# First weights from ScalarE's queue, products by quarter for two tiles, squares in column tiles, merged semaphores in the generator

## The reference, cut to what matters

```python
# layer 0
scale = cond @ norm_w.T + 1.0
h = x * (scale[:, None, :] * rsqrt(mean(x * x) + 1e-6))
val, gate = split(h @ up_w.T)            # 2 x 1024 columns
h = val * gelu(gate)
y = act_quant(h) @ weight_quant(down_w).T + x
# layer 1: gamma * rmsnorm(x) + beta goes into attention, and again into
# silu(x @ gate_w.T) * (x @ hidden_w.T) @ out_w.T + out_b
```

## Time and profile before

| | us |
|---|---|
| median of 3 runs | 745.24 (744.87 to 746.19) |
| the profiled execution | 745.31 |
| its span | 743.5 |
| TensorE busy, share of the span | 98% |
| VectorE, ScalarE, GpSimd busy | 69%, 49%, 55% |

### The profile page before, as it was taken

The page is one execution under the profiler, slowest core; times in us unless marked ns, Lnnn a source line. Parts: engine busy times, 40 slices in busy tenths (PEclk is TensorE's granted clock), DMA queues, the critical chain, the costliest instruction groups (busy, mean ns, idle before and its releaser), DMA issues.

```text
span 743.5 us, 18090 instructions
## 1 busy us (share of the span) xinstructions
PE 728.1 (98%) x6406; PEld 596.1 (80%) x6406; DVE 515.2 (69%) x806; ACT 361.3 (49%) x721; POOL 410.6 (55%) x408
## 2 busy tenths in 40 slices
PE   8999999999999899999999999999999999999996
PEld 7788888888888799999998777777777767778884
DVE  3987777777789889888985464646655567454467
ACT  3544443444447687888875333333333332322585
POOL 4646545555678888999987624224242423320344
PEclk9999999999999999999999999999999999999998
DMA  8954443454433010000004355577757777769953
GB/s 277 272 108 107 107 107 101 103 120 120 102 71 72 15 34 3 2 1 0 2 4 121 98 173 177 175 229 207 209 172 257 206 218 234 235 166 387 386 179 129
DMA packets 81002, 105.71 MB, mean 142 GB/s; under 512 B 39824, under 2 KB 53296, under 8 KB 80816
## 3 DMA queue, kind: packets, MB, share of 16 engines
q1 hardware_dynamic: 79792, 103.33, 47.2%
q10 hardware_dynamic: 1152, 1.59, 0.8%
HBM read 75.24 MB, written 21.26 MB: 130 GB/s over the span
## 4 chain that ended last, share of the span: by engine, by line
PE 89%; DVE 3%; POOL 3%; DMA 2%; issue 2%; ACT 1%; SPq 0%; DVEq 0%; POOLq 0%; ACTq 0%
PE banks L1283 22%; PE banks L440 22%; PE banks L1313 12%; PE banks L1129 5%; PE banks L1335 4%; PE banks L1206 4%; PE banks L521 4%; PE banks L1164 3%; PE banks L1247 3%; PE banks L1222 2%; PE banks L1944 2%; PE banks L1188 2%; PE banks L1914 2%; DMA qt<-q 1%; DMA early<-in_up_t 1%
## 5 line engine op out<-in xcount | busy, mean ns | idle before, releaser
L620 ACT ACTIVATE gelu<-banks,rstd 128x512 f32<-128x512 f32 x64 | 44.0, 688 | 116.5 <-PE banks L440 114.8
L1665 DVE TENSOR_TENSOR g<-banks,silu 128x512 f32<-128x512 f32 x64 | 44.1, 690 | 78.9 <-PE banks L1283 49.4
L1505 ACT ACTIVATE g_hi<-g 128x512 fp32r<-128x512 f32 x64 | 40.4, 631 | 96.9 <-DVE g L1665 95.9
L1669 DVE TENSOR_TENSOR g_lo<-g,g_hi 128x512 fp32r<-128x512 f32 x64 | 54.5, 852 | 47.5 <-ACT g_hi L1505 47.5
L1499 ACT ACTIVATE silu<-banks 128x512 f32<-128x512 f32 x64 | 38.2, 597 | 96.7 <-PE banks L1283 96.7
L440 PE MATMUL banks<-up_hi,xs_hi 128*128 128x512 f32 x256 | 81.9, 401 | 1.4 <-POOL xs_lo L370 0.8
L440 PE MATMUL banks<-up_lo,xs_hi 128*128 128x512 f32 x256 | 79.0, 391 | 0.4 <-DVE up_lo L774 0.4
L440 PE MATMUL banks<-up_hi,xs_lo 128*128 128x512 f32 x256 | 79.2, 391 | 0.0
L1283 PE MATMUL banks<-mlp_in_hi,w_hi 128*128 128x512 f32 x252 | 78.8, 393 | 0.0
L1283 PE MATMUL banks<-mlp_in_lo,w_hi 128*128 128x512 f32 x252 | 78.0, 391 | 0.0
L1283 PE MATMUL banks<-mlp_in_hi,w_lo 128*128 128x512 f32 x252 | 77.8, 390 | 0.0
(11 more groups left out here) (224 smaller groups left out, 1791.9 us busy)
## 6 DMA issues: line engine op xcount, KB each, us to landing
gen_hyper<-in_gen_t SPq DMA_DIRECT2D x32, 512.0 KB, 4.5
gen_made<-base_w SPq DMA_DIRECT2D x64, 256.0 KB, 4.6
adapter_w<-gen_made SPq DMA_DIRECT2D x64, 256.0 KB, 4.4
tokens<-in_x_tok SPq DMA_DIRECT2D x32, 128.0 KB, 2.3
w_stage<-in_w_t SPq DMA_DIRECT2D x32, 128.0 KB, 2.5
tokens_again<-in_x_tok SPq DMA_DIRECT2D x32, 128.0 KB, 2.3
weight_slot<-adapter_w SPq DMA_DIRECT2D x4, 1024.0 KB, 8.9
x_sb<-in_x_t SPq DMA_DIRECT2D x7, 512.0 KB, 7.0
```

The source lines that it names most:

```text
L620: nc.scalar.activation(gelu[:, j, :], up_bank(s, j, 1)[:, :], ACT.Gelu, scale=rstd0[:, bass.ds(s.at(0), 1)]).then_inc(Z["gelu_done"], 1)
L1505: nc.scalar.activation(gs[0][:, f % 2, :], g[:, f % 2, :], ACT.Copy).then_inc(S["g_hi_done"], 1)
L1665: nc.vector.tensor_tensor(g[:, f % 2, :], chunk_bank(s, f, 1)[:, :], silu[:, f % 2, :], ALU.mult).then_inc(S["g_done"], 1)
L1669: nc.vector.tensor_tensor(gs[1][:, f % 2, :], g[:, f % 2, :], gs[0][:, f % 2, :].bitcast(FP32), ALU.subtract).then_inc(S["g_ready"], 1)
```

## The change

The first up piece is loaded as two quarters by ScalarE's queue, together with the two small conditioning loads; SyncE begins with the tokens and the second piece. TensorE's first products go by these quarters, and the second tile's products move forward. The warm-up products are 7 and 9 instead of 14 and 7. ScalarE squares the first tokens behind the second piece, not the first.

```diff
-        sp.dma_start(cond_t[:], io["cond_t"]).then_inc(Z["loaded_norm"], 16)
-        sp.dma_start(cond_w[:, NORM * P:(NORM + 1) * P], ...).then_inc(Z["loaded_norm"], 16)
         load_x(0, 256, "loaded_x0")
-        load_up(0)
+        load_up(1)
         load_tokens(first[0])
-        load_up(1)
         load_up(2)
         load_up(3)
...
+    def load_first_up(act):
+        act.dma_start(cond_t[:], io["cond_t"]).then_inc(Z["loaded_norm"], 16)
+        act.dma_start(cond_w[:, NORM * P:(NORM + 1) * P], ...).then_inc(Z["loaded_norm"], 16)
+        for d, loaded in enumerate((Z["loaded_first"], loaded_up[0])):
+            act.dma_start(up_f[:, d, AT0:AT0 + 512], io["up_t"][:, d, AT0:AT0 + 512]).then_inc(loaded, 16)
...
+        pe.wait_ge(Z["xs_hi_done"], 1)
+        for d in range(DH):
+            pe.wait_ge(Z["up_hi_done"], d + 1)
+            nc.tensor.matmul(up_bank(first, J0, PART0)[:, :], xs_hi[:, 0, d, :], up[0][:, d, AT0:AT0 + 512], start=d == 0, stop=False)
         pe.wait_ge(Z["xs_ready"], 1)
-        pe.wait_ge(Z["up_hi_done"], 1)
-        with_high(first, 0)
+        up_product(first, 0, 1, 0, False, False)
...
         pe.wait_ge(Z["xs_ready"], 2)
         with_high(second, 0)
+        with_low(second, 0)
+        pe.wait_ge(Z["up_hi_done"], DONE0 + 1)
+        with_high(first, 1)
+        pe.wait_ge(Z["up_lo_done"], DONE0 + 1)
+        with_low(first, 1).then_inc(Z["up_done"], 1)
+        with_high(second, 1)
...
-        warm(WARM)
+        warm(WARM // 2)
         pe.wait_ge(Z["loaded_norm"], 32)
         cond_vector(NORM, norm_ps, 0).then_inc(Z["norm_ready"], 1)
-        warm(WARM // 2)
+        warm(WARM // 2 + 2)
```

```diff
-                        last = nc.tensor.matmul(bank[3][:, 0:GTA], core["ones"][:], sq[:, d, :], start=d == 0, stop=d == DH - 1)
+                        for b in range(GBA):
+                            last = nc.tensor.matmul(bank[3][32 * b:32 * b + 32, 0:L], core["ones"][:, 0:32], sq[:, d, b * L:(b + 1) * L],
+                                                    start=d == 0, stop=d == DH - 1)
...
-                    st = stat[:, bass.ds(s.at(5) * GTA, GTA)]
+                    st = early_rstd[:, s.at(5), :]
...
+            for t in range(KEPT):
+                sp.wait_ge(A["ss_ln_done"], t + 1)
+                sp.dma_start(rstd_row[t * GTA:(t + 1) * GTA].rearrange("(b l) -> b l", b=GBA), early_rstd[0:P:32, t, :]).then_inc(Z["row_stored"], 16)
+                if t % 2:
+                    sp.wait_ge(Z["row_stored"], 16 * (N0 // 4 + t + 1))
+                    wait(sp, A["early_spread"], 8 * (t - 1))
+                    part = slice((t - 1) * GTA, (t + 1) * GTA)
+                    sp.dma_start(stat[:, part], rstd_row[part].unsqueeze(0).to_broadcast([P, 2 * GTA])).then_inc(A["early_spread"], 16)
```

```diff
                 if s.live(0):
                     pair = s.at(0)
+                    wait(sp, S["made_stored"], 64 * pair)
                     for k in range(2):
-                        wait(sp, made_stored[k], 32 * pair)
...
                         for k in range(2):
                             ve.wait_ge(S["gen_done"], 2 * pair + k + 1)
-                            ve.wait_ge(base_copied[k], 32 * pair + 32)
+                            ve.wait_ge(S["base_copied"], 64 * pair + 64)
```

More of the change, by code:

```diff
@@ L664, in body @@
                 attention_input_high(nc, act, core, 0, 0)
+        load_first_up(act)
         nc.scalar.preload_act_table_set("gelu_and_others")
-        for i, (j, part) in enumerate(UP_ORDER):
+        act.wait_ge(Z["loaded_first"], 16)
+        nc.scalar.activation(up[0][:, 0, AT0:AT0 + 512], up_f[:, 0, AT0:AT0 + 512], ACT.Copy).then_inc(Z["up_hi_done"], 1)
+        act.wait_ge(loaded_up[0], 16)
+        nc.scalar.activation(up[0][:, 1, AT0:AT0 + 512], up_f[:, 1, AT0:AT0 + 512], ACT.Copy).then_inc(Z["up_hi_done"], 1)
+        for i, (j, part) in enumerate(UP_ORDER[1:], 1):
             at = part * FF + j * 512
@@ L770, in vector_program @@
             nc.vector.tensor_scalar(cond[:, NORM, m, :], norm_ps[m], 1.0, None, ALU.add).then_inc(Z["norm_done"], 1)
-        for i, (j, part) in enumerate(UP_ORDER):
+        for d in range(DH):
+            ve.wait_ge(Z["up_hi_done"], d + 1)
+            nc.vector.tensor_tensor(up[1][:, d, AT0:AT0 + 512], up_f[:, d, AT0:AT0 + 512],
+                                    up[0][:, d, AT0:AT0 + 512].bitcast(FP32), ALU.subtract).then_inc(Z["up_lo_done"], 1)
+        for i, (j, part) in enumerate(UP_ORDER[1:], 1):
             at = part * FF + j * 512
-            ve.wait_ge(Z["up_hi_done"], i + 1)
+            ve.wait_ge(Z["up_hi_done"], DONE0 + i)
             nc.vector.tensor_tensor(up[1][:, :, at:at + 512], up_f[:, :, at:at + 512],
@@ L989, in body @@
                             sp.dma_start(adapter_w[:, bass.ds(half * P // 2 * GEN_N + (2 * pair + k) * 2 * GEN_N, 2 * GEN_N)],
-                                         made[B * half:B * (half + 1), k].rearrange("p q n -> p (q n)")).then_inc(made_stored[k], 16)
+                                         made[B * half:B * (half + 1), k].rearrange("p q n -> p (q n)")).then_inc(S["made_stored"], 16)
                 if s.live(0):
                     pair = s.at(0)
+                    wait(sp, S["made_stored"], 64 * pair)
                     for k in range(2):
-                        wait(sp, made_stored[k], 32 * pair)
                         for half in range(2):
@@ L1003, in _ @@
             pipeline(sp, GEN_CALLS // 2, 1, 2, body)
-            for k in range(2):
-                sp.wait_ge(made_stored[k], 32 * (GEN_CALLS // 2))
+            sp.wait_ge(S["made_stored"], 64 * (GEN_CALLS // 2))
             sp.wait_ge(S["rows_stored"], 16 * (NS - 2))
@@ L1742, in _ @@
             output_low(d1)
+            ve.wait_ge(Z["row_stored"], 16 * (N0 // 4 + KEPT))
             gated(s1, 0)
```

44 lines of the change are left out of this document (20 added, 24 removed).

## The result

The changed kernel takes 746.35 us (median of 22 runs, 745.12 to 748.01), the kernel before 745.30 in the same session (22 runs, 744.28 to 746.66). The ratio is 1.0016 with a 95% interval of 1.0011 to 1.0022: +1.2 us, 0.8 to 1.6. I had forecast 745.0, a few tenths less than before. The direction was wrong. The time lies inside the wide range (742.4 to 748.3), which says little, and just outside the forecast's own (744.0 to 746.3). All executions behind the numbers of this text are in the fast state; one execution of the changed kernel in e16 took 2525 us and is left out. The changed kernel's profiled execution took 746.71, its span 744.9, against 745.31 and 743.5 before.

What follows compares the result with a forecast made beforehand. TensorE was taken to bound the kernel, holding 89% of the chain. 745.31 - 0.9 (start) - 0.6 (squares) + 1.2 (merged semaphores) = 745.0 us; wide range 742.4 to 748.3, the forecast's own 744.0 to 746.3.

Steps and rivals of the forecast that it cites:

- Start, -0.9: At the start, `qt` lands 0.9 us earlier and sets the first down product; TensorE's 2.8 us lead mostly becomes waiting.
- my limit of 8: Sign for the start: first real product expected at about 7.1 us; part 1 wrong if later than 8.
- Squares, -0.6: In four attention tiles, column tiles save 1.6 us on TensorE, but one becomes a wait for GpSimd's `p_sb`: -0.6 us.
- A tile's squares: Squares on TensorE: 0.68 us per tile before, 0.28 expected from L1222's instructions; under 0.35 was the sign of being right.
- Merged semaphores, +1.2: In the generator, SyncE waits for all four stores and VectorE for all four loads; TensorE loses 1.2 us.
- The hole at 528: In the generator, TensorE wants a product at 528.67 that VectorE finishes at 529.5: loss 0.9 us.
- the four pairs after it: Generator pairs at 13.5 to 15.5 us, inheriting 1.5 to 2.5 us of lateness each: 0.2 us put for them.
- my tolerance: In the generator, a chunk without a residual lets VectorE be some 3.6 us late.
- Rival C: Merged waits in the generator cost nothing, the loop staying under 11.6 us: 743.8 us; chance 0.09.
- Rival A: The generator's loop falls behind, deciding from 14.7 us per loop on: loss 4.5 instead of 1.2, 748.3 us; chance 0.22.
- Rival B: At the start `qt` comes with TensorE, whose lead mostly survives: -2.6 instead of -0.9, 743.3 us; chance 0.25.
- Rival D: Squares in the attention give their full 1.6 us because GpSimd has slack: 744.0 us; chance 0.02.

Runs made afterwards that it cites:

- e16: The changed kernel, unchanged, timed again beside the kernel before: 746.26 us, ratio 1.0017.
- e13: The kernel before, unchanged, timed against itself: 745.38 to 745.07 us, ratio 0.9999.
- e2: The kernel before with the merged generator semaphores alone: 746.64 us against 745.05 for the kernel before, ratio 1.0015.
- e11: Changed kernel, generator semaphores per half, GpSimd normalising the second half of `p_sb` earlier in the last peeled step: 744.33 us against 745.40 for the kernel before.
- e1: The changed kernel with its generator semaphores per half again: 744.73 us against 745.05 for the kernel before, ratio 0.9997.

## Why the prediction was wrong, step by step

- **Start, -0.9.** The place was right: TensorE waits for `qt`, 1.3 to 1.6 us in five of nine profiled executions of this start, and is not let through with its lead; in the other four `qt` was in, and TensorE began at 28.9 to 29.1, each time 0.1 behind the end of VectorE's `downq`. The numbers on the way were not: the first real product at 8.96, outside my limit of 8, because the first quarter was not rounded before 8.19 and the warm-up products were not through, and the third tile at 20.22 instead of 19.6. The size rested on one execution of before, whose first down product was the latest of seven, and I named nothing as late next, where VectorE's chain stood right behind. Alone the start measures -0.7; with the squares behind it, the pair is worth about -0.3 where I had -1.5.
- **Squares, -0.6.** This step failed. I compared TensorE with the first half of `p_sb` and took the 0.6 between 301.65 and 302.23 for free room. The second half, two rows further down GpSimd's timeline (302.77 and 1.93, so 304.70, and 304.74 with the 0.04 for the semaphore), had 0.09 us of room before the transpositions at 304.83. The other way in which GpSimd sets these steps, by ScalarE's `k_sb`, I did not look for; and its rows are not quite back to back, for each step holds 0.87 us of waiting for ScalarE's rounding. Alone the tiles shorten the attention by 0.2 to 0.3; on top of the new start they lengthen it by 0.3 to 0.5 (159.25 to 159.58 and more), which is a loss that I had excluded. It stands at the scores of 320 and 340, and its cause stays open.
- **A tile's squares** took 0.36 where L1222 gave 0.28. The Trainium skill (TensorEngine Tiling (Array Packing), Key Properties) says that changing the tiling mode drains the array; 0.08 us per tile for two changes of mode would agree with it, though no run here separates the two, and the row of L1222 has such changes on both sides as well.
- **Merged semaphores, +1.2.** The mechanism, the pairs and the first hole were right: nine pairs where I said seven, waits of 0.5 to 2.9. The term was too small: +1.8 in the generator's column against the kernel before (means of two, 297.82 and 295.99) and +2.1 against all kernels with waits per half, about +1.5 by the runs. The hole at 528 cost 0.4 where I priced 0.9; but the one behind pair 11 (601.86) cost 0.6 where I priced 0.1, and the four pairs after it 0.95 where I priced 0.2 (TensorE goes from 0.13 early to 0.46 and then 1.41 late). The 0.95 go in one place, at 622.91, where TensorE waits for the low half (L1696), a step that my tolerance left out and that took 2.48. Another 0.3 went at 549, at a wait for `y_alpha` that the kernel before has too (0.2 and, in e13, 0.9). Rival C is out: the merged waits are not free. Rival A's loop ran at 13.8 to 14.7 us, at the edge from which I said it would decide, and brought about half of its price.
- **Rival B** did not come in the time. In the changed kernel's first profile `qt` needed 7.27 us again; in four of the nine executions it took 5.0 to 6.2, and TensorE began the down product at 28.9 to 29.1, but nothing like the -2.6 reached the end. Rival D's full saving exists (1.22, since a tile saves 0.32 and not 0.40), but only behind a lighter GpSimd.

The sum by the runs: about -0.3 for start and squares, +1.5 for the waits, +1.2. Against the forecast (-1.5 and +1.2) nearly all of the miss is gains that I counted, and a third of a microsecond cost. The table's columns, two executions each, divide it more evenly: -0.5 before the attention where I had -0.9, +0.1 in it where I had -0.6, +1.8 in the generator where I had +1.2. That the time lies inside the range all the same is not to the credit of the sum.

**What stays open.** The start alone measures -0.7 twice, yet in the traces the attention begins no earlier with it. Some 0.3 of it lies in the attention's column; the rest is not located. And -0.7 for the start with about -0.3 for both would mean that the squares cost something on top of it. The attention's column says so in every trace (0.3 to 0.5); the intervals of 0.7 of the runs alone don't prove it.

## What to carry to other kernels

When two engines are nearly in balance, check every wait of the step against the engine that doesn't get faster, not just the first; the tightest one (here 0.09 us) decides what a saving is worth. A semaphore merged over two halves costs what the later half's landing adds, at both ends of the loop, and it shows where the loop is dense and the engine's next instructions are long. Before a term of under 1 us is built on the time at which one transfer landed in one execution, profile the same kernel again: here the same start code moved that point by 1.2 us.

## What the runs showed of the hardware

- The granted clock falls after waits that look harmless. After holes of 2.26 us (e2) and 1.60 us (e11) TensorE ran at 0.52 and 0.50 of its full clock for 2 to 3 us (the lower level is 1.2 GHz) and lost another 1.7 and 1.6 us; after 1.40 (the changed kernel) and 1.61 us (e1) at the same place as e11's it did not. So a lead that ends in a wait can end as a loss. The Trainium skill (TensorE: Matmul & The Clock Gate, Part 1) says that the clock goes by how busy the array has lately been, and that the point where it turns varies from run to run. The traces agree with the second: a hole of 1.60 us was followed by the fall, one of 1.61 us at the same place was not.
- The same `qt` transfer took 5.0 to 7.6 us behind the token loads, over 16 executions, and 3.2 in both with half of them moved behind it.
- The two 256 KB quarters on ScalarE's queue, issued 0.6 us apart beside SyncE's loads, landed at 7.54 and 8.53, 5.9 and 6.3 us after their issue.
- VectorE's low half `g_lo` (128x512) took 0.69 us in all 44 instructions of the changed trace that had none of GpSimd's work beside them, or under 0.1 us of it, and 0.69 to 2.74 us in the 20 that had.
